# Flamingo block on one Trainium2 core: key rows packed in halves and quarters of tiles, one subtraction moved to GpSimd, work order rewritten

## What is computed

```python
# cross attention, 8 heads of width 128
f_q, f_k, f_v = proj(layernorm(x)), proj(ctx), proj(ctx)          # LN, then @ w_in.T
cosine = (f_q . f_k) / (|f_q| |f_k|)
var    = q_ratio[:, None] * k_ratio[None, :]
mixed  = cw * cosine + vw * cosine * decorr_scale + ww * var      # no softmax over the keys
x = x + tanh(g_xattn) * ((mixed @ f_v) @ w_out.T + b_out)
# feed-forward: attention with 16 heads of width 16 (the softmax runs over the queries)
n = layernorm(x);  z = attention(n @ Wq, n @ Wk, n @ Wv) @ Wo
x = x + tanh(g_ffn) * gelu(l2norm(l2norm(z) @ Wff))
```

## Time and profile before

| | before |
|---|---|
| median of 3 runs | 1363.93 us (1363.42 to 1369.82) |
| the profiled execution | 1365.88 us, its span 1364.4 us, granted clock 0.978 |
| PE busy | 1259.7 us, 92% |
| DVE busy | 1113.5 us, 82% |
| ACT busy | 1026.6 us, 75% |
| POOL busy | 191.5 us, 14% |

### The profile page before, as it was taken

The page is one execution under the profiler, slowest core; times in us unless marked ns, Lnnn a source line. Parts: engine busy times, 40 slices in busy tenths (PEclk is TensorE's granted clock), DMA queues, the critical chain, the costliest instruction groups (busy, mean ns, idle before and its releaser), DMA issues.

```text
span 1364.4 us, 35000 instructions
## 1 busy us (share of the span) xinstructions
PE 1259.7 (92%) x10770; PEld 799.1 (59%) x10770; DVE 1113.5 (82%) x3164; ACT 1026.6 (75%) x3398; POOL 191.5 (14%) x130
## 2 busy tenths in 40 slices
PE   4999788999999999999999999999999999999864
PEld 2667556666656565657575657565656566665521
DVE  6986656897979797979797979798989889797854
ACT  5766233687878797979697979787888878787886
POOL 2352120102020202020100101010101020202000
PEclk9999899999999999999999999999999999999977
DMA  8440011606050515151414232332415060605140
GB/s 256 146 145 19 11 35 39 206 5 207 16 193 30 173 49 169 54 169 54 159 63 129 94 122 101 98 125 76 147 52 171 22 200 1 210 13 176 34 155 16
DMA packets 163127, 141.25 MB, mean 104 GB/s; under 512 B 9326, under 2 KB 150799, under 8 KB 163088
## 3 DMA queue, kind: packets, MB, share of 16 engines
q1 hardware_dynamic: 163088, 140.76, 31.8%
HBM read 87.00 MB, written 42.55 MB: 95 GB/s over the span
## 4 chain that ended last, share of the span: by engine, by line
PE 60%; DVE 14%; issue 11%; ACT 1%; POOL 1%; DVEq 0%; ACTq 0%; POOLq 0%; PEldq 0%
PE work L893 16%; PE work L895 15%; PE work L894 15%; PE attended L1393 8%; PE score L1382 4%; DVE nm L1674 4%; PE work L1285 2%; DVE Vpl L1571 2%; DVE l2s L1643 1%; DVE x2S L1637 1%; DVE xTl L1590 1%; DVE wqTl L1576 1%; DVE qst L1596 1%; PE work L1332 1%; ACT oTh L1488 0%
## 5 line engine op out<-in xcount | busy, mean ns | idle before, releaser
L1481 ACT ACTIVATE prob<-score,nm 128x256 f32<-128x256 f32 x1024 | 477.5, 499 | 41.9 <-DVE nm L1674 41.0
L1674 DVE TENSOR_REDUCE nm<-score 128x2 f32<-128x512 f32 x512 | 337.4, 681 | 11.1 <-PE score L1382 10.8
L1481 ACT ACTIVATION_READ_ACCUMULATOR prob<-score,nm 128x1 f32 x1024 | 238.6, 233 | 0.0
L1596 DVE BATCH_NORM_STATS2 qst<-work 128x6 f32<-128x128 f32 x512 | 112.5, 284 | 94.0 <-PE work L895 94.0
L1393 PE MATMUL attended<-prob,vsp 128*32 128x256 f32 x2048 | 138.9, 396 | 14.2 <-DVE vsp L1689 12.9
L1382 PE MATMUL score<-qstack,kstack 64*128 64x256 f16 x1024 | 99.7, 279 | 15.6 <-ACT prob L1481 13.5
L1528 POOL TENSOR_TENSOR rq<-qft,mhalf 128x32 f32<-128x32 f32 x16 | 86.8, 5427 | 164.4 <-DVEq L1603 164.4
L893 PE MATMUL work<-woutTh,fvph 128*128 128x256 f16 x384 | 105.2, 274 | 2.1 <-DVE Vpl L1571 1.1
L894 PE MATMUL work<-woutTl,fvph 128*128 128x256 f16 x384 | 104.7, 273 | 0.0
L895 PE MATMUL work<-woutTh,fvpl 128*128 128x256 f16 x384 | 104.7, 273 | 0.0
L893 PE MATMUL work<-wTh,xTh 128*128 128x512 f16 x256 | 97.5, 381 | 2.0 <-DVE xTl L1590 2.0
(11 more groups left out here) (327 smaller groups left out, 3220.9 us busy)
## 6 DMA issues: line engine op xcount, KB each, us to landing
qstack<-parts SPq DMA_DIRECT2D x64, 256.0 KB, 3.6
kstack<-parts SPq DMA_DIRECT2D x64, 256.0 KB, 4.1
sqE<-sq_rows SPq DMA_DIRECT2D x64, 154.0 KB
s_xin<-in_x SPq DMA_DIRECT2D x8, 1024.0 KB, 6.0
xin<-in_x SPq DMA_DIRECT2D x16, 512.0 KB, 3.8
x2S<-in_x SPq DMA_DIRECT2D x16, 512.0 KB, 3.4
parts<-qh SPq DMA_DIRECT2D x32, 256.0 KB, 2.4
parts<-ql SPq DMA_DIRECT2D x32, 256.0 KB, 2.5
```

The source lines that it names most:

```text
L1481: nc.scalar.activation(prob[:, g % PG, e, j + jj, :], sc[n % SC][:, jj * NQ:(jj + 1) * NQ], ACT.Exp, bias=nm[:, u + jj:u + jj + 1], accum_ ...
L1596: last = nc.vector.bn_stats(qst[:, t, 4 * half + h, :], bank(e)[:, h * DH:(h + 1) * DH])
L1674: nc.vector.tensor_reduce(nm[:, u:u + 2], sc[n % SC][:, :].rearrange("p (u q) -> p u q", q=NQ), AX.X, ALU.max, negate=True).then_inc(max_r ...
```

## The change

Key rows are laid out anew. Of each head's 77 rows, 64 go into half a tile (heads 2t and 2t+1 share tile t, for t = 0 to 3) and the other 13 into a quarter-head slot of 16 rows of a fifth tile. So each matmul of `V` and `d` writes 64 or 32 rows of a PSUM tile, with a weight load of 64 or 32 columns, and two or four of them fill one tile. `fvp` and `G` get strides of 96 and 80 with zeros between.

- `V`: 36 matmuls of 128 columns for a batch become 24 of 64 and 24 of 32 columns. `d`: 30 become 48 of 64 and 24 of 32. `G`: chunks of two heads, 8 chunks where there were 6.
- The variance and bias rows leave tile 5 and get tiles of their own, `mE` and `vE`; `y` has a sixteenth matmul (of one product) for each 256-column output. `a1.h` writes two copies on ACT; the `wq` DMAs go, `ldr` has 3 DMAs instead of 2.
- `a0` transposes factors that `qs2` has already repeated 16 times (512 values for each partition where there were 32), so that ACT writes the fifth tile of `sqE` itself. `sqe0` and `sqe1` are 4 DMAs each.
- `m.l` goes from DVE to POOL, as a plain subtraction: the factor 64 of `m.h` now sits in `sqE`.
- `ORDER` is a new list.

```diff
-rk V0 qs1 V1 V0.h ldx V0.l S0 qpow V1.h G0 M0 V2 G0.h V1.l X0 M1 a1 V2.h S1 G0.l a1.h V2.l X1 G1 M2 G2 M3 G1.h S2 G2.h
-a1.l X2 G1.l G3 qs2 X3 G2.l a0 M4 V3 a0.v M5 G3.h aux R0 X4 ldy G3.l S3 z V3.h G4 G5 X5 P0 V3.l G4.h sqe0 G5.h S4 M6
-V4 M7 X6 G4.l X7 M8 V5 wq G5.l V4.h S5 M9 d0 X8 R1 M10 X9 P1 V4.l V5.h M11 sqe1 S6 X10 fk0 V5.l M12 X11 M13 fk1 E0
...
-L3 pq1.l O2 O1. parts1 O3 O2. q2 O3. back0 q3 F1 q2.o pv0 q3.o F2 back3 q4 pv0.v back1 q5 q4.o back2 F3 q6 q5.o q7
-q6.o pv1 q7.o F4 pv1.v out res
+rk S0 S1 qs1 G0 V0 G0.h V1 V0.h V1.h G0.l qpow M0 a1 V0.l a1.h V1.l G1 X0 M1 G2 G1.h a1.l G2.h X1 G1.l V2 M2 G2.l V2.h
+S2 G4 X2 M3 G3 V2.l G4.h qs2 G3.h X3 G4.l a0 M4 a0.v M5 S3 X4 V3 aux G3.l ldx R0 G5 V3.h M6 G6 P0 G5.h M7 X5 V3.l G6.h
+S4 G5.l X6 G7 sqe0 G6.l V4 M8 X7 V5 M9 ldr G7.h S5 R1 V4.h G7.l P1 M10 V5.h ldy X8 V4.l d0 X9 M11 sqe1 V5.l fk0 X10
+d0.o z S6 fk0.h fk1 m0.h M12 m0.l d1 fk0.l fk1.h X11 fk1.l d2 M13 X12 d3 R2 X13 d1.o d2.o S7 E0 S8 m1.h M14 d4 m2.h
+m1.l M15 X14 L0 d5 m2.l X15 d3.o P2 d4.o m3.h M16 m4.h zT0 m3.l M17 S9 X16 y0 R3 X17 d5.o m4.l M18 zT0.h M19 m5.h X18
+m5.l zT0.f P3 y0.o X19 zT0.l zT1 S10 zT1.h S11 M20 y1 E1 M21 X20 L1 R4 zT1.f M22 X21 M23 X22 zT1.l O0 y1.o X23 ln1 fk2
+O0. S12 P4 fk2.h M24 lpow q0 M25 X24 R5 X25 ln2 S13 P5 fk2.l zz0 E2 q0.o zz1 zz0.h M26 zz1.h q1 zz0.l X26 zz1.l S14
+M27 pq0 q1.o X27 M28 pk0 pq0.h M29 X28 pq0.l S15 X29 pk1 M30 M31 X30 pq1 R6 X31 L2 P6 pk0.h R7 pk1.h pk0.l P7 pq1.h
+pk1.l parts0 O1 E3 L3 pq1.l O2 O1. O3 O2. q2 O3. back0 q3 F1 q2.o parts1 q4 q3.o F2 q5 back2 q6 q4.o F3 q5.o q7 q6.o
+pv0 q7.o pv1 pv0.v F4 pv1.v res back3 out back1
...
+def value_block(h, b2):
+    return FS * (2 * h + b2) + LEFT * (h % 2)
+def left_block(h, b2):
+    return FS * (2 * h + b2) + (64 if h % 2 == 0 else -16)
...
+                        if t < HT - 1:
+                            for m, (x, y) in enumerate(("hh", "hl", "lh")):
+                                for h in (2 * t, 2 * t + 1):
+                                    at = value_block(h, b2)
+                                    last = nc.tensor.matmul(bk[64 * (h % 2):64 * (h % 2) + 64, cols], fvp[x][:, at:at + 64],
+                                                            w["woutT"][y][:, h, :], start=m == 0, stop=m == 2)
+                            continue
+                        for odd in range(2):
+                            for m, (x, y) in enumerate(("hh", "hl", "lh")):
+                                for j in range(H // 2):
+                                    at = left_block(2 * j + odd, b2)
+                                    last = nc.tensor.matmul(bk[32 * j:32 * j + 32, cols], fvp[x][:, at:at + 32],
...
+                            for m, (x, y) in enumerate(("hh", "hl", "lh")):
+                                for row, size, at in key_tile(t, b2):
+                                    last = nc.tensor.matmul(bk[row:row + size, n * 2 * P:(n + 1) * 2 * P], G[x][:, k, at:at + size],
...
+                        last = nc.tensor.matmul(bk[:, r * DIM:(r + 1) * DIM],
+                                                mE[0:Y_ROWS, c * NQ + r * P:c * NQ + (r + 1) * P], vE[0:Y_ROWS, c, :],
+                                                start=False, stop=True)
...
+                    nc.scalar.activation(mE[0:H, :], bank(e)[0:H, :], ACT.Copy, scale=MS)
+                    nc.scalar.activation(mE[LL_ROW:LL_ROW + H, :], bank(e)[0:H, :], ACT.Copy, scale=MS).then_inc(hi_ready[lead(e)], 1)
...
+                elif e[0] == "m":
+                    if e.endswith(".l"):
+                        step, done = e[:-2], HALVES[lead(e)]
+                        pool.wait_ge(hi_ready[lead(e)], a * len(done) + done.index(step) + 1)
+                        dst, src, _ = emptied(step, "l")
+                        nc.gpsimd.tensor_tensor(dst, src, emptied(step, "h")[0], ALU.subtract).then_inc(m_ready, 1)
...
-                    nc.vector.tensor_tensor(aux[:, 0, :, :], rq[:], bc(w["cvec"][:].unsqueeze(1), [P, PT, H]),
+                    nc.vector.tensor_tensor(auxq[:].rearrange("p t (h i) -> p t h i", h=H), bc(rq[:].unsqueeze(3), [P, PT, H, 16]),
+                                            bc(w["cvec"][:].unsqueeze(1).unsqueeze(3), [P, PT, H, 16]),
                                             ALU.mult).then_inc(sq_ready, 1)
```

More of the change, by code:

```diff
@@ L41 @@
 HM_TILES = [(0, 1), (2, 3), (4,)]
-HM_ROWS = [min(P, HM - P * t) for t in range(HT)]
-KR_ROW = HM_ROWS[-1]
-ONE_ROW = KR_ROW + H
-Y_ROWS = HM_ROWS[:-1] + [ONE_ROW + 1]
 SB = NB // NG
@@ L996, in half @@
     return group, e, 2 * i, 2 * (4 * group + 2 * e + i)
-def window(t, h, b2):
-    return PAD * (2 * h + b2) + 127 + P * t - MK * h
-def tile_heads(t):
-    return [h for h in range(H) if MK * h < P * (t + 1) and MK * (h + 1) > P * t]
-SQ_LOADS = [sum(len(tile_heads(t)) for t in part) for part in ((0, 1), (2, 3, 4))]
+def value_block(h, b2):
+    return FS * (2 * h + b2) + LEFT * (h % 2)
+def left_block(h, b2):
+    return FS * (2 * h + b2) + (64 if h % 2 == 0 else -16)
+SQ_LOADS = [4, 4]
 def main_phase(nc, ctx, w, x_rows, out_rows, rk_rows, kr_rows, sq_rows, fixed_rows, parts):
@@ L1030, in main_phase @@
     rk_all, rkc = sb("rk_all", [P, HT, NB]), sb("rkc", [P, HT, 2])
[L1031 removed]
+    aux, auxq = sb("aux", [P, PT, H]), sb("auxq", [P, PT, P])
     st4, qst, qft = sb("st4", [P, PT, 2]), sb("qst", [P, PT, H, 6]), sb("qft", [P, 5, PT, H])
@@ L1102, in key_cols, with key_tile @@
     def key_cols(half, lo_h, hi_h):
-        return fvp[half][:, 0:2 * H * PAD].rearrange("p (n c) -> p n c", c=PAD)[:, 2 * lo_h:2 * hi_h, 127:PAD]
+        return fvp[half][:].rearrange("p (n c) -> p n c", c=FS)[:, 2 * lo_h:2 * hi_h, 0:MK]
+    def key_tile(t, b2):
+        if t == HT - 1:
+            return [(32 * j, 32, GS * (4 * j + 2 * b2) + 64) for j in range(H // 2)]
+        return [(64 * odd, 64, GS * (4 * t + 2 * b2 + odd) + LEFT * odd) for odd in range(2)]
     def emptied(e, half):
@@ L1331, in a_part @@
                     for t in range(PT):
-                        last = nc.tensor.transpose(bk[0:H, t * P:(t + 1) * P], aux[:, c, t, :], ident[:])
+                        if c == 0:
+                            last = nc.tensor.transpose(bk[:, t * P:(t + 1) * P], auxq[:, t, :], ident[:])
+                        else:
+                            last = nc.tensor.transpose(bk[0:H, t * P:(t + 1) * P], aux[:, t, :], ident[:])
                 elif kind == "y":
```

161 lines of the change are left out of this document (80 added, 81 removed).

## The result

The changed kernel takes 1378.73 us (median of 5 runs, 1378.46 to 1381.03), the kernel before 1363.93 (1362.46 to 1369.82) beside it: a ratio of 1.0095, 95% interval 1.0072 to 1.0118. Faster by 10 us was forecast, and it is slower by 13 to 15. The profiled execution takes 1378.64 us; its span is 1376.8 us against 1364.4, its mean granted clock of TensorE 0.960 against 0.978.

The account below looks back on a forecast made before the run. ACT was taken to bound each turn up to S4, PE behind it. 14 turns losing 0.55 us (7.7) plus 2.5 for turns 1 and 16 gave 1355.7 us profiled, 1353.7 median; range 1336 to 1380 (8 in 10).

Parts of the forecast that it names:

- The price of the column tiles: In V and d: full overlap, two matmuls of 64 columns or four of 32 in 0.11 us.
- rival 3: Column tiles don't overlap fully in float16: a quad takes 0.25 us, kernel 1402 us, 1378 at half that penalty; chance 14%.
- PE saved ahead of S4 only becomes a wait: V0 to V3: 27 of 36 saved slots lie where ACT leads, so they don't count in full.
- ScalarE sets the pace up to S4: Turn's start to S4: S4 waits for ACT's X5; S4 at 14.2 instead of 14.56 us, counted as -0.4 us.
- rival 2: The coupling eats PE's saving: DVE and ACT within 3 us of PE in 56.7; time 1361 us, 1357 to 1371; chance 17%.
- those 4 us of waiting: Expected sign: PE waits about 4 us between a1 and S4, with ACT dense before S4.
- the term that was forecast as -0.15: Behind S4: change in a turn between -0.15 and +0.44 us, taken as -0.15.
- y's 0.44: Behind S4: y's 60 matmuls become 64, adding 0.44 us of PE work to a turn.
- P5's wait: Behind S4: PE's 0.59 us wait for P5's values hangs on DVE's R5; most of it was expected to go.
- What is late next is PE itself: Behind S4: with most of the 0.59 us wait at P5 gone, PE itself is the next limit.
- d, priced at 0: Step d: 30 slots of PE stay 30, so no gain.
- Turns 1 and 16: The same V work without one of the other leads: 2.5 us saved together, bounds 0 and 5.

Follow-up runs that it names:

- the two mixed kernels: Changed kernel with the old list of steps, ratio 1.0415; kernel before, packing and engines untouched, with the new list, ratio 1.0358.

## Why the prediction was wrong, step by step

For the profiled execution 1355.7 us was forecast and 1378.64 came, 22.9 us more. Three terms of about the same size make up 22.7 of them: the turn without a fall of the clock, 71.04 us instead of 70.45 (8.3 us over 14 turns); the falls of the clock, for which the sum had no term (8.1 us); and what lies ahead of and behind the full turns (6.3 us).

- **The price of the column tiles was right.** A pair and a quad take 0.11 us; rival 3 is out. The Trainium skill, TensorE: Matmul & The Clock Gate, section Part 1, with its 25 ns between two starts agrees: four start within 0.11 us.
- **"PE saved ahead of S4 only becomes a wait" was right for the kernel before**, and stronger than stated: it holds up to S5 (half of V taken out: 0.00). I had put the border at S4. In the changed kernel there are two exceptions: V2 is on the path (0.7 us more of it made S4 0.38 to 0.68 us later), and S5 follows S4 after 2.38 us instead of 2.80, so part of what V4 and V5 save may have been kept there; how much, no run shows.
- **The step "ScalarE sets the pace up to S4" was wrong.** I read that S4 waits for X5. In the earlier trace rows it starts right behind P0, and X5 ended about 0.5 us earlier. VectorE leads there, up to `G3.l`. In the changed kernel it is VectorE up to `a1.l`, then V2, then ScalarE from `V2.h` on. `qs2`'s 0.68 us, which I had costed and then left out as covered, were on the path with 0.25. So S4 at 14.10, where I had 14.2, with 3.7 us of PE idle ahead of it, where I had about 4, was partly luck: a right number from a sum over the wrong queue. (ACT is also 4.0 us below PE in the 56.72 us of the earlier trace rows, not within 3 as rival 2 says.)
- **The step that I didn't take: what those 4 us of waiting do to the clock.** The kernel before has no fall of the granted clock in the full turns of its trace, and I treated waits as free. Ten of 14 turns ran 3.4 us at 1.2 GHz behind them, and the work that is slowed then was on the path: 8.1 of the 12.5 us. The price is shown, by turns with and without a fall in one execution. That the waits bring the falls is supported by the table, and by the kernel before with half of V, where nothing else was changed; it isn't shown by a kernel that fills them.
- **Behind S4: 56.94 us instead of 56.3, the term that was forecast as -0.15 and measured +0.49.** y's 0.44 was right (7.11 against 6.67 us). P5's wait went, as expected. But I expected it to go without a successor, and the new list has others: from P5's last matmul to the next start 0.63 us instead of 0.31, and 0.30 instead of 0.11 behind the transposes that follow. "What is late next is PE itself" was wrong there: the transposes wait for VectorE's `ln2`. d, priced at 0, costs 0.27 us a turn (7.17 against 6.90). The rival that the coupling eats the saving is the one nearest to what a turn without a fall did.
- **GpSimd: right in the full turns.** A subtraction of 512 values takes 1.16 us by the row below, of after's timeline, and no wait on it shows there. The Trainium skill, GPSIMD Engine Reference, section Performance versus the Vector engine, gave 1.1 by the estimate; the trace agrees. In the short turn ahead of the first full one VectorE did wait for it, 1.7 and 1.4 us. What I missed is that it isn't only hidden but needed: 0.93 us a turn.

```profile
561.89 1.16 POOL L1566 TENSOR_TENSOR mTl<-md,mTh 128x512 f16<-128x512 f32 x1 [15.42 <-ACT mTh L1484]
```

- **Turns 1 and 16: -2.5 us forecast, +3.4 ahead of the loop and +0.4 behind it.** I had read no row of these. 2.4 of the 3.4 us are in the block of q there, which runs at a mean granted clock of 0.88 instead of 1.00; PE is idle 4.4 of the 8 us ahead of it (2.8 of 7 before). That the list does most of it is what the two mixed kernels say; which of its steps is open.
- The range (1336 to 1380) held the time, but the side was wrong, and no rival had this cause.

What stays open: why the falls come in some turns and not in others that are alike up to then, and the 2.0 us stand at the jump. The kernel before has one trace only; its executions beside these runs took 1362 to 1372 us at mean granted clocks of 0.982 to 0.971, and whether the longer ones have falls in full turns isn't known. No version here beats the kernel before. The nearest, m.l on GpSimd alone, is level with it.
